# Both weighted sums of a block issued back to back in a fused cross-attention and spectral feed-forward kernel

## The reference

```python
q, k, v = layernorm(x) @ wq + bq, ctx @ wk + bk, ctx @ wv + bv      # split in 16 heads
score = einsum('bhqd,bhkd->bhqk', q, k) / sqrt(32) * mask
score = where(score == 0, -1e9, score)
context = einsum('bhqk,bhkd->bhqd', softmax(score), v)              # the weighted sums
x = x + context @ wo + bo
x = x + real(ifft(fft(layernorm(x)) @ (w_real + 1j * w_imag))) + bias
```

## Time and profile before

| | |
|---|---|
| median of 3 runs | 437.13 us (437.1 to 437.85) |
| the profiled execution, its own time | 437.16 us |
| its span, first to last instruction | 435.4 us |
| PE busy | 429.1 us, 99% of the span |
| PE weight loads | 297.3 us, 68% |
| DVE busy | 398.4 us, 92% |
| ACT busy | 365.1 us, 84% |
| POOL busy | 355.6 us, 82% |
| TensorE clock granted | 1.0 of full speed |
| chain that ended last | PE 90%, DVE 4%, POOL 2%, issue 2%, ACT 1% |

### The profile page before, as it was taken

How to read it: one execution, slowest core, us unless ns; L and a number is a source line. 1 busy time by engine, 2 the same in 40 slices (tenths; PEclk the granted TensorE clock), 3 DMA queues, 4 the chain that set the end, 5 groups by cost and what they waited for, 6 DMA issues and landing times.

```text
span 435.4 us, 10922 instructions
## 1 busy us (share of the span) xinstructions
PE 429.1 (99%) x3496; PEld 297.3 (68%) x3496; DVE 398.4 (92%) x533; ACT 365.1 (84%) x1340; POOL 355.6 (82%) x484
## 2 busy tenths in 40 slices
PE   7999999999999999999999999999999999999997
PEld 6897788686776676666677667766676765556544
DVE  3899799999999999999999999999999899999663
ACT  1768997889988998999898998998998899999720
POOL 5779988868999898989889898989899865665693
PEclk9999999999999999999999999999999999999999
DMA  8999954404545655445454545445542434331144
GB/s 269 396 387 256 305 167 125 107 0 110 128 108 123 168 95 161 102 124 140 128 147 130 132 112 153 92 136 145 110 104 63 108 79 112 75 88 49 50 110 132
DMA packets 85286, 60.15 MB, mean 138 GB/s; under 512 B 40141, under 2 KB 72813, under 8 KB 84718
## 3 DMA queue, kind: packets, MB, share of 16 engines
q1 hardware_dynamic: 84508, 59.29, 50.0%
q10 hardware_dynamic: 722, 0.17, 0.2%
HBM read 29.33 MB, written 8.39 MB: 87 GB/s over the span
## 4 chain that ended last, share of the span: by engine, by line
PE 90%; DVE 4%; POOL 2%; issue 2%; ACT 1%; POOLq 0%; DVEq 0%
PE bank L478 34%; PE bank L483 24%; PE bank L641 11%; PE bank L655 6%; PE scores L627 5%; PE bank L584 3%; PE bank L565 2%; PE scores L483 1%; DVE zs L968 1%; ACT zs L744 1%; PE bank L661 1%; PE bank L491 1%; DVE zs L961 1%; POOL cl L1256 1%; DVE x L946 0%
## 5 line engine op out<-in xcount | busy, mean ns | idle before, releaser
L744 ACT ACTIVATE zs<-zs,nbias 128x128 f32<-128x128 f32 x512 | 199.8, 397 | 13.9 <-POOL nbias L1243 13.5
L744 ACT ACTIVATION_READ_ACCUMULATOR zs<-zs,nbias 128x1 f32 x512 | 99.5, 194 | 0.0
L968 DVE SCALAR_TENSOR_TENSOR zs<-zs 128x1024 f32<-128x1024 f32 x64 | 89.0, 1390 | 1.1
L973 DVE TENSOR_REDUCE nmin<-zs 128x8 f32<-128x1024 f32 x64 | 78.1, 1220 | 2.1
L961 DVE TENSOR_TENSOR zs<-scores,ms 128x1024 f32<-128x1024 f32 x64 | 78.0, 1218 | 0.1
L753 ACT COPY pt<-bank 128x512 f32<-128x512 f32 x128 | 67.9, 582 | 8.2 <-PE bank L641 8.0
L641 PE MATMUL bank<-ident,zs 128*128 128x128 f32 x512 | 66.7, 273 | 0.1
L1195 POOL TENSOR_TENSOR xs<-xs,bob 128x512 f32<-128x512 f32 (+1 forms) x41 | 43.4, 1059 | 22.9 <-DVE zs L968 22.8
L483 PE MATMUL bank<-xth,wqh 128*128 128x256 f16 x224 | 61.2, 273 | 0.0
L483 PE MATMUL bank<-xtl,wqh 128*128 128x256 f16 x224 | 61.1, 273 | 0.0
L483 PE MATMUL bank<-xth,wql 128*128 128x256 f16 x224 | 61.1, 273 | 0.0
(11 more groups left out here) (128 smaller groups left out, 903.9 us busy)
## 6 DMA issues: line engine op xcount, KB each, us to landing
xs<-in_x SPq DMA_DIRECT2D x16, 512.0 KB, 4.3
xtr<-in_xt SPq DMA_DIRECT2D x16, 512.0 KB, 4.6
out<-x SPq DMA_DIRECT2D x31, 256.0 KB, 2.5
qs<-qh SPq DMA_DIRECT2D x120, 64.0 KB
lp<-in_lparts SPq DMA_DIRECT2D x4, 1024.0 KB, 10.3
qs<-ql SPq DMA_DIRECT2D x60, 64.0 KB
ms<-in_mask SPq DMA_DIRECT2D x16, 128.0 KB, 2.5
wks<-in_wk SPq DMA_DIRECT2D x2, 512.0 KB, 6.5
```

Source lines behind the costliest of these rows:

```text
L744: last = act.activation(z, z, ACT.Exp, bias=nbias[:, s % 4, i:i + 1], scale=-NEG, accum_out=zsum[:, s % 4, i:i + 1])
L968: dve.scalar_tensor_tensor(out=z, in0=z, scalar=0.0, in1=z, op0=ALU.is_equal, op1=ALU.subtract).then_inc(eq_done, 1)
L973: dve.tensor_reduce(nmin[:, s % 4, :], zs[:, s % NZ].rearrange("p t h k -> p (t h) k"), AX.X, ALU.min).then_inc(mn_done, 1)
```

## The change

In blocks 3 to 12 (`PAIRED`) the sum of the even half is no longer issued in slot 4c + 3 but in slot 4c + 5, right before that of the odd half, as a fill "P" in a rotating bank. Its ctx_norm, ctx_hi and ctx_lo move from slot 4c + 5 to slot 4c + 6; ctx_norm reads the rotating bank and counts it free. pt gets a second buffer, ptb, at the place of a start-up weight; odd halves use it in all blocks, and copy_pt waits for the sum two halves back. The counters of the sums that stay in CX are adapted (`own`).

```diff
+PAIRED = range(3, 13)
...
+        both = [("P", (v - 5) // 4)] if r == 1 and (v - 5) // 4 in PAIRED else []
         base = len(fills)
-        fills += mid + late
+        fills += mid + both + late
...
+        items += [("G", base + len(mid))] * len(both)
-        if v % 2 == 1 and 0 <= v - 3 < NS:
+        if v % 2 == 1 and 0 <= v - 3 < NS and not in_fill((v - 3) // 2):
             items += [("PV", (v - 3) // 2)]
...
+def in_fill(m):
+    return m % 2 == 0 and m // 2 in PAIRED
+
+def own(m):
+    return m + 1 - sum(in_fill(i) for i in range(m + 1))
...
+        ptb, _ = sb("ptb", [128, 2, 4, CH], F32, a_wv)
+        pts = [pt, ptb]
...
+                elif kind == "P":
+                    last = weighted(2 * c, o)
...
-            def weigh(m):
+            def weighted(m, o):
                 c, h = divmod(m, 2)
                 b = c // (NC // NB)
                 pe.wait_ge(pt_copied, 4 * m + 4)
-                if m >= 1:
-                    pe.wait_ge(cn_done, m)
-                else:
-                    pe.wait_ge(g_free, at["V", 0] + 1)
...
-                        last = pe.matmul(CX[32 * j:32 * j + 32, 256 * i:256 * i + 256], vs[:, b, n:n + 32],
-                                         pt[:, i, j, :], start=True, stop=True)
-                last.then_inc(pv_done, 1)
+                        last = pe.matmul(o[32 * j:32 * j + 32, 256 * i:256 * i + 256], vs[:, b, n:n + 32],
+                                         pts[m % 2][:, i, j, :], start=True, stop=True)
+                return last
+
+            def weigh(m):
+                if m >= 1:
+                    pe.wait_ge(cn_done, own(m) - 1)
+                else:
+                    pe.wait_ge(g_free, at["V", 0] + 1)
+                weighted(m, CX).then_inc(pv_done, 1)
...
-                if f == 0 and s >= 2:
-                    act.wait_ge(pv_done, s // 2)
-                act.copy(pt[:, s % 2, 2 * f:2 * f + 2, :], PB[f][:]).then_inc(pt_copied, 1)
+                if f == 0 and s >= 4:
+                    wait_weighed(act, s // 2 - 2)
+                act.copy(pts[s // 2 % 2][:, s % 2, 2 * f:2 * f + 2, :], PB[f][:]).then_inc(pt_copied, 1)
...
-                if v % 2 == 1 and 0 <= v - 5 < NS - 2:
+                if v % 2 == 1 and 0 <= v - 5 < NS - 2 and not in_fill((v - 5) // 2):
                     ctx_hi((v - 5) // 2)
+                if v % 2 == 0 and in_fill((v - 6) // 2):
+                    ctx_hi((v - 6) // 2)
...
-                dve.tensor_tensor(cn[:], CX[:].rearrange("p (i n) -> p i n", i=2), rec[:], ALU.mult).then_inc(cn_done, 1)
+                src, done = (bank_of(at["P", m // 2]), g_free) if in_fill(m) else (CX, cn_done)
+                dve.tensor_tensor(cn[:], src[:].rearrange("p (i n) -> p i n", i=2), rec[:], ALU.mult).then_inc(done, 1)
```

More of the change, by code:

```diff
@@ L87, in plan @@
             late.append(("QQ", (v + 9) // 4, (v + 9) % 4 // 2))
+        both = [("P", (v - 5) // 4)] if r == 1 and (v - 5) // 4 in PAIRED else []
         base = len(fills)
-        fills += mid + late
+        fills += mid + both + late
         mids = list(range(base, base + len(mid)))
-        lates = list(range(base + len(mid), len(fills)))
+        lates = list(range(base + len(mid + both), len(fills)))
         items = []
@@ L294, in cast_count, with wait_weighed, wait_context @@
             return n + 1 - min(n + 1, 2) - min(max(n + 1 - tile_of(12, 0), 0), 4)
+        def wait_weighed(eng, m):
+            if in_fill(m):
+                eng.wait_ge(g_done, at["P", m // 2] + 1)
+            else:
+                eng.wait_ge(pv_done, own(m))
+        def wait_context(eng, m):
+            if in_fill(m):
+                eng.wait_ge(g_free, at["P", m // 2] + 1)
+            else:
+                eng.wait_ge(cn_done, own(m))
         def columns(n):
@@ L758, in copy_rec @@
                 if m >= 1:
-                    act.wait_ge(cn_done, m)
+                    wait_context(act, m - 1)
                 act.copy(rec[:], bank_of(n)[:].rearrange("p (i n) -> p i n", i=2)).then_inc(rc_done, 1)
@@ L763, in ctx_hi @@
                 c, h = divmod(m, 2)
-                act.wait_ge(cn_done, m + 1)
+                wait_context(act, m)
                 if h == 0 and c >= 2:
@@ L982, in ctx_norm @@
                 dve.wait_ge(rc_done, m + 1)
-                dve.wait_ge(pv_done, m + 1)
+                wait_weighed(dve, m)
                 if m >= 1:
                     dve.wait_ge(p_cl, m)
-                dve.tensor_tensor(cn[:], CX[:].rearrange("p (i n) -> p i n", i=2), rec[:], ALU.mult).then_inc(cn_done, 1)
+                src, done = (bank_of(at["P", m // 2]), g_free) if in_fill(m) else (CX, cn_done)
+                dve.tensor_tensor(cn[:], src[:].rearrange("p (i n) -> p i n", i=2), rec[:], ALU.mult).then_inc(done, 1)
             def last_ctx_lo():
@@ L1091, in _ @@
                     recip(NS // 2 - 1)
-                if v % 2 == 1 and 0 <= v - 5 < NS - 2:
+                if v % 2 == 1 and 0 <= v - 5 < NS - 2 and not in_fill((v - 5) // 2):
                     ctx_norm((v - 5) // 2)
+                if v % 2 == 0 and in_fill((v - 6) // 2):
+                    ctx_norm((v - 6) // 2)
                 for n in prompt:
@@ L1408, in _ @@
                     norm_lo2(c - 2, 0)
-                elif v % 2 == 1 and 2 <= v - 5 < NS - 2:
+                elif v % 2 == 1 and 2 <= v - 5 < NS - 2 and not in_fill((v - 5) // 2):
                     ctx_lo((v - 5) // 2)
+                if v % 2 == 0 and in_fill((v - 6) // 2):
+                    ctx_lo((v - 6) // 2)
                 if v == NS + 1:
```

## The result

The changed kernel takes 442.3 us (median of 6 runs) against 437.65 us for the kernel before in the same runs: a ratio of 1.011, interval 1.0093 to 1.0127. The forecast was 442.2 us, slower. The profiled execution took 442.08 us, with a span of 440.3.

A forecast was written before the change was run, and what follows sets the result against it. PE bounds the kernel before, at 24.10 us a block; after the change a loop over PE, ACT and DVE of 24.66 binds. Terms -0.62 + 8 x 0.56, -0.23, +0.87, +0.51 give +5.01: 442.2 us, range 438.4 to 444.0.

The forecast's parts named there:

- The loop over PE, ACT and DVE: Scores(38) through transposes, copy, query cast, ql and mask_mul(41) to scores(42): from 23.28 to 24.66 us, 0.56 more per paired block.
- the bracket: In the way from ql of slot 38 to mask_mul(41): 14.26 less 0.20 us idle before 273.76, giving 14.06.
- PE's wait of about 0.8 us for mask_mul: Sign of being right: PE waits this long per paired block, ahead of the scores of odd slots 21 to 49.
- PE's saving: Two sums back to back spare PE one entering and leaving of tiled mode: 0.23 us in each of 10 blocks.
- The second buffer: Second buffer of turned weights: ACT's copies never wait for a sum, so it gives nothing by itself.
- zero_to_neg of slot 40 stays at 1.67: DVE's zero_to_neg there still meets POOL's add_bo and takes 1.67 us; the other bound was 1.22.
- The second rival: POOL falls out of zero_to_neg's way in slot 4c+8: loop 24.21, whole +1.4, 438.6 us; chance 0.15.
- The first loop: PE's lead of 1.10 us from the sum taken out of slot 15 is cut at scores(18) to 0.62.
- the fourth rival's wait: One more wait, ctx_lo of the odd half against slot 40's WO tile or FF against ql's bank: 443 to 444 us; 0.07.
- The sum: Over the kernel: +3.86 us by scores(50), then +3.63, together +5.01 us; with the median 437.13 gives 442.2 us.
- the last three terms: Slots 50 to 53 give 0.23 us back; second sum in slot 53 adds 0.87; ctx_hi in slot 54 adds 0.51.
- The rival "PE stays the bound": Ten blocks give 0.23 us each, the 0.51 in slot 54 stays: -1.8 us, 435.4 us; chance 0.12.

The follow-up runs named there:

- Run 1: Changed kernel with ACT's query cast ahead of ctx_hi of the even half in slots 4c+6: 437.91 us, ratio 0.9999 to the kernel before.
- run 7: Changed kernel with the even half's sum computing only 8 of 16 matmul records, 0.43 us less on PE: 439.78 us, ratio 1.0049 to the kernel before.
- best: Changed kernel with query cast before ctx_hi, POOL's spread and half add_bo after zero_to_neg, half split_lo after bias: 435.84 us, ratio 0.9954 to the kernel before.
- run 8: Changed kernel with pairing in blocks 3 to 7 only: 439.89 us, ratio 1.0056; with no block paired, second buffer kept: 437.83 us, ratio 1.0006.
- run 2: Changed kernel with POOL's spread and first half of add_bo held until the next slot's zero_to_neg ends: 443.48 us, ratio 1.0131 to the kernel before.
- run 3: Changed kernel, query cast before ctx_hi and POOL's spread and half add_bo after zero_to_neg: 438.57 us; also with the query tile between the sums: 438.99 us.
- run 5: Kernel before, sums not paired, with the same two POOL moves as best: 439.94 us, ratio 1.0048 to the kernel before.
- run 6: Kernel before with useless 0.51 us ACT casts ahead of the query cast in slots 18, 22 ... 54: two casts 444.57 us, one cast 439.59 us.

## Why the prediction was right, and where it was not

- **The loop over PE, ACT and DVE** (24.66 forecast, 24.57 measured). All its terms but one came out within 0.01 us: 5.05, 0.63, 3.02, 0.61. The way from ql to mask_mul(41) was 13.97, not 14.06: of the wait before ql of slot 40, 0.29 went away instead of the 0.20 in the bracket. The bracket counts from the end of `least`, but without a wait ql starts before that end (276.42 to 277.56 in the changed kernel, 1.14 us, where `least` lasts 1.22). That is a size, 0.09 a loop. Run 1 takes ACT's share out of the loop and the period follows in full (0.52 for 0.51); run 7 takes 0.43 of PE's share out and the period follows by 0.26, down to the second loop.
- **PE's wait of about 0.8 us for mask_mul**, named as a sign of being right, did not show in that form: PE gives up 0.71 us a block, but 0.30 of it at ctx_lo, 0.32 at the reciprocals and only 0.06 at mask_mul. The length of the loop was right, the place of the waits was not.
- **PE's saving** (0.23 a block): 0.24 against the old order, shown in best and in the last paired blocks of the changed kernel (23.86). In the changed kernel it is hidden but for those.
- **The second buffer** at nothing: run 8.
- **zero_to_neg of slot 40 stays at 1.67**: row at 274.72. The second rival, which hung on it, did not come.
- **The first loop.** Here a step failed. The forecast has PE 0.62 us ahead at scores(18), cut by mask_mul(17) alone. Measured from scores(13), to leave out a start that was 0.62 us later in this execution (105.28 against 104.66), the lead was 0.14. PE's timeline of the changed kernel shows two waits that I had priced at nothing:

```profile
126.34 0.38 PE L505 MATMUL bank<-woh,ch 128*128 128x512 f16 x1 [0.49 <-POOL cl L1293]
...
128.93 0.61 PE L656 MATMUL scores<-ks,qs 102*128 102x128 f16 x8
129.68 0.63 PE L611 MATMUL bank<-ident,rzb 128*128 128x128 f32 x4
```

  A PE that gets ahead by 1.11 us runs into ctx_lo of the odd half (the fourth rival's wait), and then into the reciprocals, which start 0.75 instead of 0.44 us after the scores. The first I had named, the second not. In the later blocks both are there again (0.30 and 0.32 us, see above) and cost nothing on top, since they are taken out of the time by which PE is ahead of mask_mul.
- **The sum.** By the same measure scores(50) are 3.47 us late (forecast 3.86), scores(54) 3.24 (3.63), mask_mul(55) 4.62 (5.01): the difference of 0.39 comes of 0.27 more at scores(22) (forecast -0.06, measured +0.21) and then 0.09 less in each of the seven loops that follow, up to rounding; the last three terms, -0.23, +0.87 and +0.51, are exact. Up to the end 0.3 is regained, so the pairing costs 4.3 us of span. The other 0.6 of 4.9 is the later start, which was not forecast. The start is scatter: scores(13) lie between 104.65 and 105.90 us in the profiled executions of all these kernels. That 442.2 and 442.3 agree so well is luck in two parts: without the late start the sum would have been 0.7 us too high, and it was added to 437.13, where the kernel before had 437.65 in the runs of the comparison; the medians differ by 4.65 us, the sum says 5.0.
- **What I overlooked**: the second loop, over POOL's bias and without PE. It is 23.8 us in the kernel before (0.3 under PE's 24.10, though longer than the first loop's 23.28) and 24.3 in the changed one, 0.26 under the first loop's 24.57, so it did not alter the time; but it spoilt the expectations of runs 2, 3, 5 and 6. It could have been guessed from the rows of before: ACT's copy at 258.54 has no idle time noted ahead of it, unlike the one at 246.55, so ACT's chain from POOL's bias was about as late as PE's transposes. My forecast used that copy as proof of a tie to PE alone.
- **The rival "PE stays the bound"** would have been right with three moves of order on ACT and POOL: best is that case, and its 435.84 lies 1.95 us under the kernel before in the same runs (437.79), against the 1.8 that the rival named. That the two are close is luck: the rival subtracts 0.5 us for the cast in slot 54, which best does not pay, and leaves out what the next row shows.
- **Why best gains less than ten blocks of 0.24** (2.4 us): in slot 16 its WO tile follows the transposes by 1.53 us (125.44 to 126.97) instead of 0.87. PE, ahead by the sum taken out of slot 15, waits 0.66 us for ctx_lo there, once. 2.4 - 0.66 = 1.74; from scores(13) on the profiled execution gains 1.79.

```profile
126.97 0.38 PE L505 MATMUL bank<-woh,ch 128*128 128x512 f16 x1 [0.49 <-POOL cl L1293]
```

Not settled: how much of POOL's contention could be removed by a better order than the one tried.

## What to carry to other kernels

When an instruction is moved, don't ask only whether its engine has idle time in the new slot, but what is queued right behind it and who waits for that: here 0.5 us ahead of the one cast that another engine was waiting for cost some 4.4 us, and behind it nothing that could be measured. An engine that is busy for 99% of the span can be replaced as the bound by a loop over engines at 82 to 92% each; close every loop round one period (cut out the idle times) before a change, and close all of them, since the second one decides what a cure is worth. The waits in the profile tell where the bounding engine stands still, not which value is late: follow that value back. Uneven slots count: moving work from one slot to another on the bounding engine changes nothing in its total, yet shifts what hangs on it.

## What the runs showed that I had not expected

zero_to_neg (1024 fp32 values, both inputs the same SBUF tile) took 1.22 us with POOL idle, and 1.34, 1.39, 1.67, 1.79 or 2.23 us where a POOL instruction on wide tiles was still running when it began. The more of that was left, the longer it took: with 0.59 us left 1.67, with 0.71 left 1.79, with 1.15 left 2.23, each time 1.08 us more than what was left. POOL's copy of 0.61 us, begun during zero_to_neg, took 1.61 in turn. Moving POOL's work away from one such meeting made two others longer, and the sum of three was 4.40 us instead of 4.22 (run 2 against the changed kernel). Here contention was moved, not removed.
